# Inverse standard deviations beside attention: ScalarE's root and a reciprocal, or a halved-bits guess and three Newton steps on VectorE

## What is computed

```python
x = L0_attn_x
h = _layernorm(x, axis=-1) * (1 + ca) + sa
x = x + ga * _L0_attn_ref(h, L0_attn_W_qkv, L0_attn_W_o)
h = _layernorm(x, axis=-1) * (1 + cb) + sb        # 1 / sqrt(var + 1e-05)
x = x + gb * _L0_ffn_ref(h, L0_ffn_router_w, L0_ffn_w1, L0_ffn_w2)
```

## Time and profile before

| | us |
|---|---|
| median of 3 runs | 2924.07 |
| lowest and highest | 2919.78, 2924.98 |
| the profiled execution | 2921.07 |
| its span in the profile | 2919.2 |
| PE busy | 2572.5 (88%) |
| DVE busy | 2203.4 (75%) |
| ACT busy | 1733.7 (59%) |
| POOL busy | 639.4 (22%) |

### The profile page before, as it was taken

The page is one execution under the profiler, slowest core; times in us unless marked ns, Lnnn a source line. Parts: engine busy times, 40 slices in busy tenths (PEclk is TensorE's granted clock), DMA queues, the critical chain, the costliest instruction groups (busy, mean ns, idle before and its releaser), DMA issues. The chain is left out here.

```text
span 2919.2 us, 49352 instructions
## 1 busy us (share of the span) xinstructions
PE 2572.5 (88%) x16192; PEld 1303.7 (45%) x16192; DVE 2203.4 (75%) x5295; ACT 1733.7 (59%) x3557; POOL 639.4 (22%) x665
## 2 busy tenths in 40 slices
PE   6886899999899999988999988899988569999990
PEld 5771333333333333333333333333332459999990
DVE  6987898888788788868878887887841657777771
ACT  3660277777567666656766665666667137777770
POOL 1224332100010101011010110101011235555553
PEclk8995699999999999999999999999999679999995
DMA  3889778502304224040321403133110635555548
GB/s 138 283 290 266 284 276 291 171 13 69 92 24 99 67 56 111 16 110 32 87 81 42 111 31 95 49 71 80 32 57 34 200 109 90 90 90 90 90 75 245
DMA packets 217119, 331.29 MB, mean 113 GB/s; under 512 B 26736, under 2 KB 157296, under 8 KB 216880
## 3 DMA queue, kind: packets, MB, share of 16 engines
q1 hardware_dynamic: 137728, 170.68, 19.8%
q0 software_dynamic: 58032, 136.67, 18.1%
q10 hardware_dynamic: 21120, 20.97, 2.3%
HBM read 140.23 MB, written 187.20 MB: 112 GB/s over the span
## 5 line engine op out<-in xcount | busy, mean ns | idle before, releaser
L980 ACT ACTIVATE probs<-ps 128x512 f32<-128x512 f32 (+3 forms) x2560 | 1197.5, 539 | 767.1 <-PE ps L1260 389.4
L1004 DVE TENSOR_REDUCE early<-ps 128x1 f32<-128x512 f32 x1536 | 1005.0, 685 | 143.9 <-PE ps L1186 119.3
L1186 PE MATMUL ps<-kh,qs 96*128 96x512 bf16 (+3 forms) x2560 | 903.2, 369 | 113.7 <-DVE early L1004 54.2
L1260 PE MATMUL ps<-qs,kh 99*128 99x512 bf16 (+3 forms) x2560 | 844.3, 356 | 45.4 <-ACT probs L980 33.3
L1276 PE MATMUL ps<-probs,vs 128*32 128x512 f32 (+3 forms) x5120 | 614.3, 552 | 0.0
L1186 PEld LDWEIGHTS ps<-kh,qs 96*128 96x128 bf16 x2560 | 251.9, 100 | 753.4 <-DVE early L1004 341.6
L1000 DVE CUSTOM_DVE_ANT_0 junk<-ps,causal 128x128 bf16<-128x128 f32 (+3 forms) x1024 | 480.8, 484 | 70.3 <-PE ps L1186 61.5
L1260 PEld LDWEIGHTS ps<-qs,kh 99*128 99x128 bf16 x2560 | 249.5, 99 | 332.2 <-ACT probs L980 208.4
L916 POOL DMA_INDIRECT rows_out<-row,place_a x96 | 95.3, 992 | 1192.4 <-DVE place_a L700 1166.8
L1675 POOL DMA_INDIRECT acc<-y,to x156 | 250.1, 1603 | 125.0 <-ACT y L1730 79.2
L1264 PE MATMUL ps<-ident_b,causal_b 128*128 128x128 bf16 x1024 | 214.4, 220 | 0.0
(11 more groups left out here) (227 smaller groups left out, 2900.0 us busy)
## 6 DMA issues: line engine op xcount, KB each, us to landing
rows_out<-row POOLq DMA_DIRECT2D x129, 544.0 KB, 3.6
xg<-rows_out SPq DMA_DIRECT2D x39, 544.0 KB
v_ones<-vt SPq DMA_DIRECT2D x16, 1024.0 KB, 6.4
vs<-v_ones SPq DMA_DIRECT2D x16, 1024.0 KB, 7.2
contexts<-ctx_out SPq DMA_DIRECT2D x64, 256.0 KB
q_parts<-parts SPq DMA_DIRECT2D x32, 384.0 KB, 3.8
k_parts<-parts SPq DMA_DIRECT2D x32, 384.0 KB, 4.6
qs<-q_parts SPq DMA_DIRECT2D x64, 192.0 KB, 3.5
```

Source lines behind the costliest of these rows:

```text
L980: nc.scalar.activation(probs[u % PB][:, h, q0:TB], bank(s % SB)[:, q0:TB], ACT.Exp, scale=SCALE).then_inc(exp_done, 1)
L1004: nc.vector.tensor_reduce(early[:, h, t, k0 // CW:k0 // CW + 1], tile, AX.X, ALU.max).then_inc(max_done, 1)
L1186: nc.tensor.matmul(tile[:, 0:w], qh[a % HR][0:STACK, t * P:(t + 1) * P], kh[a % HR][0:STACK, k0:k0 + w], start=True, stop=True).then_inc(m ...
L1260: mm = nc.tensor.matmul(bank(s % SB)[:, q0:TB], kh[a % HR][:, kt * P:(kt + 1) * P], qh[a % HR][:, j * TB + q0:(j + 1) * TB], start=True, s ...
```

## The change

`deviation` writes variance plus EPS to a tile of its own, waits for it, and calls a new function `inverse_root`, which makes the inverse root by thirteen VectorE instructions on 128x4: shift the bits of the float right by one, convert to float, subtract from the constant 0x5F3759DF, convert back to integer, which read as a float is the first guess, and three times square, multiply by minus half the variance, add 1.5 and multiply. Each waits for the one before through `rstd_done`. ScalarE's `root`, its place among the scores and the reciprocal in `modulate` are gone. `block1` and `dispatch_rest` keep their roots on ScalarE.

```diff
+ROOT_ROUNDS = 3
+ROOT_STEPS = 4 + 3 * ROOT_ROUNDS
...
+        variance = sb("variance_b", [P, TT])
+        halved = sb("halved_b", [P, TT], I32)
+        guess_f = sb("guess_f_b", [P, TT])
+        square = sb("square_b", [P, TT])
...
-                def root(n):
-                    act.wait_ge(var_done, (2 * TT + 1) * (n + 1))
-                    nc.scalar.activation(rstd[:, :], rstd[:, :], ACT.Sqrt).then_inc(rooted, 1)
-
...
-                                if at == SCORES_TO[DEVIATION] + 6:
-                                    root(n)
...
+                def inverse_root(n):
+                    done = ROOT_STEPS * n
+
+                    def linked(step, ins):
+                        ins.then_inc(rstd_done, 1)
+                        dve.wait_ge(rstd_done, done + step)
+
+                    linked(1, nc.vector.tensor_scalar(halved[:, :], variance[:, :].bitcast(I32), 1, None,
+                                                      ALU.logical_shift_right))
+                    linked(2, nc.vector.tensor_copy(guess_f[:, :], halved[:, :]))
+                    linked(3, nc.vector.tensor_scalar(guess_f[:, :], guess_f[:, :], -1.0, float(0x5F3759DF), ALU.mult,
+                                                      ALU.add))
+                    linked(4, nc.vector.tensor_copy(rstd[:, :].bitcast(I32), guess_f[:, :]))
+                    for k in range(ROOT_ROUNDS):
+                        linked(5 + 3 * k, nc.vector.tensor_tensor(square[:, :], rstd[:, :], rstd[:, :], ALU.mult))
+                        linked(6 + 3 * k, nc.vector.scalar_tensor_tensor(
+                            out=square[:, :], in0=square[:, :], scalar=-0.5, in1=variance[:, :], op0=ALU.mult,
+                            op1=ALU.mult))
+                        linked(7 + 3 * k, nc.vector.scalar_tensor_tensor(
+                            out=rstd[:, :], in0=square[:, :], scalar=1.5, in1=rstd[:, :], op0=ALU.add, op1=ALU.mult))
+
...
-                    nc.vector.tensor_scalar(rstd[:, :], mv[:, :, 1], EPS, None, ALU.add).then_inc(var_done, 1)
+                    nc.vector.tensor_scalar(variance[:, :], mv[:, :, 1], EPS, None, ALU.add).then_inc(var_done, 1)
+                    dve.wait_ge(var_done, done + 2 * TT + 1)
+                    inverse_root(n)
...
-                    dve.wait_ge(rooted, n + 1)
-                    nc.vector.reciprocal(rstd[:, :], rstd[:, :]).then_inc(rstd_done, 1)
-                    dve.wait_ge(rstd_done, n + 1)
```

More of the change, by code:

```diff
@@ L749, in attend @@
         ctx_norm, o_mm, gated_done, res_done = sem("ctx_norm"), sem("o_mm"), sem("gated_done"), sem("res_done")
-        var_done, rooted, rstd_done = sem("var_done"), sem("rooted_b"), sem("rstd_done")
+        var_done, rstd_done = sem("var_done"), sem("rstd_done")
         centred_done, h2_done, token_done = sem("centred_done"), sem("h2_done"), sem("token_done")
```

## The result

The changed kernel takes 2962.11 us (median of 4 runs, 2957.29 to 2969.12), the kernel before 2924.53 in the same session (4 runs, 2919.78 to 2933.78). The ratio is 1.0137, with a 95% interval of 1.0118 to 1.0157: 37.6 us slower. The profiled execution of the changed kernel is the slowest of its four: 2969.12 us, span 2967.3, 48.1 us over the span of before. So what is read from the profile is a difference of 48.1 us, and the medians differ by 37.6.

What follows compares the result with a forecast made beforehand. VectorE was taken to set the pace in the attention stretch around the deviation step. From 2921.1 us, chain +28.2, last group −3.5 and clock +5 gave 2950.8, put at 2952 us; range 2938 to 2968.

Steps and rivals of the forecast that it cites:

- the forecast's own case: Whole kernel: chain passed on whole, with few falls of the clock; 2941 to 2962 us, chance 0.70.
- VectorE sets the pace there, and the chain is passed on whole: Blocks 0 to 10, from EPS addition to modulating: net 2.56 us a block reaches the end, +28.2 us.
- Rival 2: Blocks 0 to 10: VectorE's idle time absorbs half or more of the chain; 2932 us, or 2918 with all gone; chance 0.11.
- ScalarE's root is worth 0 in blocks 0 to 10: Attention's block groups: freeing 2.81 us of ScalarE a block gains 0, at most 0.3 us each.
- Rival 3: Every block: ScalarE is the late engine, so removing the detours gains 42 us against 28 added; 2907 us, chance 0.05.
- The last group: Group 16 with block 11: the table-load pause goes, −2.1 us, and the clock stays, about −1.4; together −3.5 us.
- The clock: Blocks 0 to 10, behind TensorE's new pause: short falls of the granted clock, 0.5 us in ten blocks, +5 us.
- its own test: Block groups: wrong if less than 1.5 us longer (absorbed) or more than 4.5 us longer (clock).
- Rival 1: Blocks 0 to 10: the clock falls in every block, nothing hides it; 31 us in place of 5, about 2977; chance 0.14.

Runs made afterwards that it cites:

- e7: The changed kernel with one Newton round instead of three, seven VectorE instructions instead of thirteen: 2942.91 us, 1.0046 of the kernel before.
- e9: The kernel before plus thirteen linked multiplications on a spare 128x4 tile at chunk 20, where TensorE sets the pace: 2937.8 us, 1.0036.
- e2: The kernel before without ScalarE's root and its table loads, and no chain in their place: 2920.73 us, 0.9993.
- e1: The changed kernel with ScalarE's root and two table loads back in their place, writing a tile nobody reads: 2979.9 us, 1.0198 of the kernel before.
- e4: The changed kernel with its thirteen operations spread over chunks 80 to 90, one or two behind each: 2948.49 us, 1.0089 of the kernel before.
- e11: The changed kernel with chunk 82's score-maximum matmul done sixteen times, so TensorE works through its pause: 2955.14 us, 1.0115 of the kernel before.
- e10: The kernel before with chunk 21's matmul done thirteen times in groups that carry a block, longer without a pause: 2948.02 us, 1.0062.
- e13: The kernel before plus fifteen linked idle GpSimd operations on a spare tile in each block, on another chip: 2882.78 us, 1.0002.

## Why the prediction was right, and where it was off

The forecast was 2952 us in a range of 2938 to 2968; 2962.1 is inside it, 10 us above the forecast, at the upper end of what the forecast's own case was given (2941 to 2962). Its own terms (chain 2.35 to 2.8 us, clock 0 to 1) add up to 2945 to 2961, so that end was reached by something that is not among them.

- **VectorE sets the pace there, and the chain is passed on whole.** Right. Forecast 2.56 us a block and 28.2 in all; measured 2.43 and 26.7 where no fall of the clock is in it. The hand-over of 35 ns taken from rows 7 held (0.20 us from start to start; six operations less are 1.18 us less in e7). Rival 2, the chain absorbed, is out: VectorE has no gap before 833.65, and e9 shows what absorption looks like where TensorE sets the pace (0.66 of 2.6 us).
- **ScalarE's root is worth 0 in blocks 0 to 10.** Right for the kernel before (e2, 0.9993). The step was incomplete, though: the worth of the root depends on the chain. Beside it the root costs 18 us (e1). So "0 for the root plus 28 for the chain" is the right sum when the root goes first; when the chain comes first, taking the root away saves 18 us. Rival 3 has fallen with e2. The trace's 2.81 us for two loads and a root showed again in e1. The Trainium skill, "ScalarE: Activation LUTs", "What ACT_TABLE_LOAD costs", adds a drain of about 1380 ns to each switch; here the root starts 0.02 us behind the load's end, so no such drain shows.
- **The last group.** Right: −3.5 forecast, −3.7 measured, by both of its parts, the pause and the clock (10.2 us low before, 6.8 now).
- **The clock: the term that was mis-sized.** The forecast was 5 us for it. In the profiled execution the block groups have up to 26 us that go with the falls (4.3 behind the chain, 22 elsewhere), by the medians about 15. Where the prediction looked, right behind the new pause, it had the size right: the fall came in every block, cost next to nothing in eight of them, and 4.3 us in all. The step that failed is that falls anywhere else in the group were put at nothing without a reason. The changed kernel has more of them 10 to 50 us later as well, from the modulating to the gate and from rank to place, where the routing's small operations leave TensorE with gaps, and there each is paid (in the kernel before a group's mod–gate takes 23.8 us, and 25.4 with one fall). The prediction named as its own test that block groups longer by over 4.5 us would mean the clock; they are 4.8 us longer. Rival 1 had the size of this about right for the profiled execution (31 against at most 26), in the wrong place and at too high a price: a single fall costs 1.6 us there, not 2.8. One of the two groups of rows 3 from which it took the 2.8 also has a longer out–end (17.3 us against 14.8). That the total stayed in the range in spite of the missing term is in part luck: the range goes up to 2968 for the sake of rival 1, whose falls are in another place.

What makes the later falls more frequent is open. The pause isn't needed for them: e4 has no pause of that size and still has 9.2 us low elsewhere in a group, where before has 5.5, and over all its runs it has some 40 us more than before. Filling the pause (e11) changed them by less than the runs scatter. A longer group as such isn't the cause (e10). Seven operations in place of thirteen (e7) leave about as many of them over all runs (432 against 408 us). The Trainium skill, "TensorE: Matmul & The Clock Gate", "HAM oscillation — how this bites in real kernels", describes a clock that drops at each gap between bursts; the row of 1.94 us behind the 2.64 us pause agrees. That rule doesn't tell of falls later on in unchanged work, which are the ones that cost most here. By a rule of one drop at one gap the change would have cost 27 us for the chain and 4 behind it, less the last group's 3.7. Why small operations spread among VectorE's reductions bring them is not shown.

## What to carry to other kernels

Before trading ScalarE time for VectorE time, find which engine sets the pace in the very stretch where each of the two stands: here 34 us of a not-late engine were worth 2 us, and 27 us of the pace-setting one cost 27 and, with the clock, nearly 40. A linked chain of tiny operations costs its latency, 0.20 us a link, and the same links between independent instructions cost half; in a stretch in which another engine is late three quarters of it vanished. When a change moves work in a loop whose TensorE has quiet stretches, compare the time at the lower clock over the whole loop, stretch by stretch and over many runs, not only right behind the new gap. And look at the single blocks behind a mean: three of eleven held nearly all of what the fall behind the chain cost.

## What the runs showed of the hardware that was not expected

- A microsecond at the lower clock costs 0.44 us on the average of this kernel's block groups. Where VectorE sets the pace, a fall of 3.4 us cost 0.0 to 0.1 us and one of 6.8 us cost 1.3: the slack there hides the short fall and not the long one.
- ScalarE, VectorE and TensorE stop together for 2 to 4 us while GpSimd issues the last indirect transfers of a block, in the profiles of some programs and not in others. One and the same program takes 2925 us on two chips and 2884 on a third, and a kernel profiled on the third has no stop; 3.7 us in each of eleven groups would be the difference. Its cause is open.
- Linked 128x4 operations on GpSimd start every 0.25 to 0.56 us, fifteen in 4.7 us, against 0.20 each on VectorE, and fifteen of them a block left the time unchanged in e13 (1.0002).
